# Adding the V bias by a one-row fp32 matmul in PSUM instead of in the VectorE eviction

## The reference, cut to what matters

```python
q = jnp.einsum('bse,hed->bhsd', x, Wq) + bq[None, :, None, :]
kg = jnp.einsum('bse,ged->bgsd', x, Wk) + bk[None, :, None, :]
vg = jnp.einsum('bse,ged->bgsd', x, Wv) + bv[None, :, None, :]
k = jnp.repeat(kg, per, axis=1)
v = jnp.repeat(vg, per, axis=1)
scores = jnp.einsum('bhqd,bhkd->bhqk', q, k) * (1.0 / np.sqrt(d))
# causal mask, softmax -> attn
out = jnp.einsum('bhqk,bhkd->bhqd', attn, v)
```

## Time and profile before

| | us |
|---|---|
| median of 2 runs | 2894.66 (2894.64 to 2894.69) |
| the profiled execution | 2895.81 |
| its span on the slowest core, core 0 | 2894.3 |
| spans of the eight cores | 2878.8 to 2894.3 |
| TensorE busy in the span (matmuls) | 1705.7 |
| ScalarE busy | 1090.4 |
| VectorE busy | 805.1 |

### The profile page before, as it was taken

One profiled execution on the slowest core, in us unless ns is written; L12 is line 12 of the kernel. 1 busy time (PEld: TensorE's weight loads), 2 busy tenths in 40 slices (PEclk: granted clock), 3 DMA queues, 4 the chain that ended last, 5 costly groups with the idle time before them and its releaser, 6 DMA issues.

```text
span 2894.3 us, 19813 instructions; the slowest of 8 cores (2878.8 to 2894.3 us)
## 1 busy us (share of the span) xinstructions
PE 1705.7 (59%) x6824; PEld 722.2 (25%) x6824; DVE 805.1 (28%) x1243; ACT 1090.4 (38%) x1040; POOL 62.2 (2%) x120
## 2 busy tenths in 40 slices
PE   0186565544434434444415888887888848788780
PEld 0033122211112112111103333333333323333330
DVE  0011000123222223223455444444444420000014
ACT  2241000599999999999451000000000000110116
POOL 0000000000000000000000000000000000000000
PEclk9998777756556556556557999999999978898895
DMA  9995322354554555555423333333333341111102
GB/s 225 264 286 132 53 36 37 102 198 169 184 190 170 188 195 174 176 189 170 150 88 117 116 117 116 117 116 117 116 111 120 117 157 39 59 57 41 59 20 116
DMA packets 50741, 376.58 MB, mean 130 GB/s; under 512 B 5588, under 2 KB 5844, under 8 KB 16724
## 3 DMA queue, kind: packets, MB, share of 16 engines
q1 hardware_dynamic: 23188, 192.32, 18.8%
q0 software_dynamic: 17088, 115.35, 14.3%
q10 hardware_dynamic: 10368, 67.64, 7.4%
HBM read 361.13 MB, written 39.32 MB: 138 GB/s over the span
## 4 chain that ended last, share of the span: by engine, by line
PE 28%; DMA 23%; ACT 19%; DVE 13%; issue 11%; another core or an unknown queue 5%; ACTq 1%; SPq 0%; DVEq 0%; POOL 0%; POOLq 0%
DMA af<-w_sb 15%; PE pH L978 12%; ACT L520 8%; DVE ab L827 7%; ACT ab L520 4%; DMA ab<-wq_sb 4%; DVE ab L824 4%; DMA ab<-w2qs 3%; ACT L399 3%; PE psB L330 1%; PE psO L330 1%; PE pH L864 1%; PE psA L330 1%; PE psR L330 1%
## 5 line engine op out<-in xcount | busy, mean ns | idle before, releaser
L864 PE MATMUL pH<-ab 128*128 128x512 bf16 x2752 | 647.7, 398 | 144.1 <-DVE ab L836 108.9
L520 ACT ACT_TABLE_LOAD x256 | 328.4, 1283 | 350.1 <-PE psA L466 309.4
L864 PEld LDWEIGHTS pH<-ab 128*128 128x128 bf16 x2752 | 275.7, 102 | 515.8 <-issue 230.9
L978 PE MATMUL pH<-ab 128*128 128x512 bf16 x1376 | 334.4, 409 | 100.2 <-DMA ab<-w2qs 100.2
L878 ACT ACTIVATE af<-pH,af 128x1024 f32<-128x1024 f32 x43 | 47.9, 1115 | 709.6 <-DVE ab L836 702.1
L824 DVE TENSOR_SCALAR ab<-af 128x2048 bf16<-128x2048 f32 x86 | 110.6, 1286 | 404.6 <-DMA af<-w_sb 404.6
L555 DVE TENSOR_TENSOR ab<-ab 128x128 bf16<-128x128 bf16 x256 | 57.5, 225 | 581.4 <-ACT ab L520 581.4
L978 PEld LDWEIGHTS pH<-ab 128*128 128x128 bf16 x1376 | 141.9, 104 | 289.0 <-issue 150.6
L827 DVE SCALAR_TENSOR_TENSOR ab<-af,ab 128x2048 bf16<-128x2048 f32 x86 | 202.3, 2352 | 9.0
L466 PE MATMUL psA<-ab 128*128 128x512 bf16 x192 | 75.8, 458 | 199.0 <-ACT ab L520 195.9
L466 PE MATMUL psB<-ab 128*128 128x512 bf16 x192 | 75.2, 455 | 167.1 <-ACT ab L520 167.0
(11 more groups left out here) (102 smaller groups left out, 1276.4 us busy)
## 6 DMA issues: line engine op xcount, KB each, us to landing
af<-w_sb POOLq DMA_DIRECT2D x86, 1024.0 KB, 5.3
af<-w_sb SPq DMA_DIRECT2D x86, 1024.0 KB, 5.0
af<-w_sb ACTq DMA_DIRECT2D x64, 688.0 KB, 5.2
af<-w_sb ACTq DMA_DIRECT2D x8, 2752.0 KB, 20.8
af<-w_sb SPq DMA_DIRECT2D x8, 2752.0 KB, 20.9
w2qs<-ab SPq DMA_DIRECT2D x16, 1376.0 KB, 8.5
ab<-w2qs SPq DMA_DIRECT2D x16, 1376.0 KB, 5.9
ab<-xkvT POOLq DMA_DIRECT2D x8, 1024.0 KB, 108.3
```

Of the source, the lines that this page charges most:

```text
L520: INC(scalar.activation(abf(A_PT + OFF[kc], N), ps[:, 0:N], AF.Exp, bias=m16col), "ex", 1)
L864: last = tensor.matmul(ps[:, b2 * 512:(b2 + 1) * 512], lhs, abf(A_XKV + ec * 1024 + b2 * 512, 512), start=(ec == 0), stop=(ec == NEC - 1))
L978: last = tensor.matmul(ps[:, b2 * 512:(b2 + 1) * 512], lhs, abf(A_G + hc * 1024 + b2 * 512, 512), start=(hc == 0), stop=(hc == NHC - 1))
```

## The change

The bias is no longer added in the eviction. A new DRAM input `bvf` (1x512 fp32) is loaded by SP, as a fourth constant counted on `ld`, into one partition of `af` at column offset `F_FSC`. Nothing else uses these columns until FFN part B. Each V unit begins with a matmul of a single contraction row: `onesrow` (1x128 fp32, all ones) is stationary and `bvf` (1x512 fp32) moves. It writes the bias to all 128 partitions of the unit's PSUM bank, with `start=True`. The 16 bf16 matmuls then accumulate on it (`start=False` throughout). The first V unit also waits for `ld`. The eviction becomes a VectorE `tensor_copy`. The bf16 replica of the bias leaves `constb`, whose size stays at 768 columns. The bias is now added in fp32 rather than rounded to bf16 first.

```diff
+    d_bv = nc.dram_tensor("bvf", [1, 512], F32, kind="ExternalInput").ap()
...
-        bvrep = abf(A_CBF + 256, 512)
...
             INC(sync.dma_start(out=abf(A_MSK, 2048), in_=d_msk), "ld", 16)
+            INC(sync.dma_start(out=af[0:1, F_FSC:F_FSC + 512], in_=d_bv), "ld", 16)
         on("sync", p0_sync)
...
-            def mk_mm(tt=tt, ps=ps):
+            def mk_mm(tt=tt, ps=ps, first=(tt == 0)):
                 def mm(tensor):
+                    if first:
+                        W(tensor, "ld", LD_CONSTS)
+                    tensor.matmul(ps[:, 0:512], onesrow,
+                                  af[0:1, F_FSC:F_FSC + 512],
+                                  start=True, stop=False)
                     last = None
                     for ec in range(NEC):
                         lhs = abf(A_XKV + ec * 2048 + tt * 128, 128)
                         last = tensor.matmul(ps[:, 0:512], lhs,
                                              abf(A_WV + ec * 512, 512),
-                                             start=(ec == 0), stop=(ec == NEC - 1))
+                                             start=False, stop=(ec == NEC - 1))
...
             def mk_ev(tt=tt, ps=ps):
                 def ev(vector):
-                    return vector.tensor_tensor(
-                        abf(A_VTM + tt * 512, 512), ps[:, 0:512],
-                        bvrep, ALU.add)
+                    return vector.tensor_copy(abf(A_VTM + tt * 512, 512),
+                                              ps[:, 0:512])
```

More of the change, by code:

```diff
@@ L1058, in _host_shared @@
     constf[:, F_EPS] = 1e-5
-    bv_cat = np.concatenate([bv[g] for g in range(GG)])
+    bv_cat = np.ascontiguousarray(
+        np.concatenate([bv[g] for g in range(GG)]).reshape(1, 512), dtype=f32)
     constb = np.zeros((128, 768), dtype=ml_dtypes.bfloat16)
@@ L1063, in _host_shared @@
     constb[:, 128:256] = np.float32(1.0)
-    constb[:, 256:768] = np.broadcast_to(bv_cat[None, :], (128, 512)).astype(
-        ml_dtypes.bfloat16)
     masks = []
@@ L1084, in _host_shared @@
     return dict(wq_sb=wq_sb, wk_sb=wk_sb, wv_sb=wv_sb, w1_sb=w1_sb, w3_sb=w3_sb,
-                w2_sb=w2_sb, constf=constf, constb=constb), masks
+                w2_sb=w2_sb, constf=constf, constb=constb, bvf=bv_cat), masks
 def kernel(L0_attn_x, L0_attn_Wq, L0_attn_bq, L0_attn_Wk, L0_attn_bk,
```

## The result

The changed kernel takes 0.78% longer: the ratio to the kernel before is 1.0078, with a 95% interval of 1.0066 to 1.0089. On 2894.28 us, the median of the kernel before in that comparison, that is 22.6 us more (19.1 to 25.8). The forecast was 13.8 us more, with the time between 2901 and 2914 us. So the direction and the small size were right, while the price was under two thirds of the measured one, and the time lies above the range. The nine executions behind the ratio go from 2913.3 to 2928.0 us; their median, 2914.5, is 20.3 us more and half a microsecond above the range. By the 2% bound the change is "same".

The account below looks back on a forecast made before the run. TensorE's unbroken V units, which gate the loads for Q, were taken as the bound. TensorE +13.8, eviction 0 and constants 0 us on the 2894.66 us median gave 2908.5 us, range 2901 to 2914 us.

Parts of the forecast that it names:

- What bounds the stage: In the V units TensorE works without idle time; a microsecond added to one moves the loads for Q and the rest.
- The eviction and the added load: VectorE's V eviction without its addition, and SP's extra 2 KB constant load: each forecast at 0 us on the path.
- Two instructions for each call, twice the bf16 time for each: Each new fp32 matmul heading a V unit: two instructions of 2 x 0.216 us, 0.86 us, 13.8 us for 16.
- The dear reading: Skill's transpose sentence read as four times the fp32 transposes' price per column, in one instruction: 28 us for 16 matmuls.
- The joins: Where bf16 matmuls and the new fp32 one meet in a V unit: no exposed weight load counted in the sum.
- the fourth of "What is added to TensorE": Bounds on the 16 new matmuls' price in the V units: 6.9 us lowest, 17.3 with exposed loads, 27.6 us upper.
- the bound for exposed loads: Both fp32 weight loads of 0.11 us exposed in each V unit: 3.5 us on top of 13.8, 17.3 us.
- Nothing given back or added later: After the V units, the loads for Q keep their 36.6 us and later stages only move, their lengths unchanged.
- exposed loads or dear columns: Rival, chance 0.17: the new matmuls in the V units cost between +17.3 and +27.6 us, total 2912 to 2922 us.
- The clock rival: Rival, chance 0.03: TensorE's clock falls to 1.2 GHz for the V units, +83 us, 2977.6 us.
- the input arrives sooner: Rival, chance 0.02: a later `w2` stream speeds the input, so time doesn't grow; it would need 13.8 us.
- the sign of 1 us around 160 us: Forecast counts as wrong if the input's last piece comes more than 1 us away from 160 us.

## Why the prediction was right or wrong, point by point

- **What bounds the stage**: right. TensorE's own time sets the end of the V units, and each microsecond there moves the loads for Q and what follows: 18.5 us more in the V units, 18.5 and 18.7 us more up to the first Q matmul. (The 33.31 us of the earlier trace rows are the last piece of that wait; from the end of the V units to the first Q matmul it is 36.6, which the sum uses.)
- **The eviction and the added load**: right, at nothing, shown by the run without the matmul. The copy costs what the addition did, 692 ns, the bound of the two at which nothing is saved.
- **Two instructions for each call, twice the bf16 time for each**: right. The full-height fp32 matmul costs 0.858 us against the forecast 0.86. The Trainium skill ("FP8 and Floating Point Precision", TensorE Precision Notes) states that true fp32 makes four passes; the 3.97 bf16 times in the table above agree with it. The dear reading, 28 us, didn't come.
- **The joins**: this step failed, the fourth of "What is added to TensorE". The sum took them at nothing, because a full-height fp32 load starts under the bf16 matmul ahead of it. The rows were right and the inference wrong: they show another type at the same height, and the new matmul differs in height as well. At full height the forecast came true to 0.1 us (13.73 against 13.8). At one row 0.30 us were added to each, 4.8 us in all, and a V unit lasted 4.61 us, over the 4.5 named as a sign of being wrong. Even the bound for exposed loads, 17.3 us, was short of 18.5: it counted the two fp32 loads at 0.11 us each, whereas one load and two waits of some 0.09 us around the change of height were lost.
- **Nothing given back or added later**: right for the loads for Q, and not quite for the rest. FFN part A was 4.2 us longer on either chip, which the sum had at nothing and the prediction named as a sign of being wrong. Its cause is open, and it isn't tied to the number of new matmuls.
- **The rivals**: "exposed loads or dear columns" came, with a chance of 0.17, at 18.5 us of its 17.3 to 27.6. Its mechanism was the right one, loads that stand exposed for another height; the prediction had itself noted that no row shows a one-row load ahead of a 128-row matmul in a dense stream. The clock rival didn't come: 1.00 through the V units. Whether the input arrives sooner can't be told to the microsecond: the V units start at 211.2 and 208.1 us in two profiles of the kernel before, and at 207.6 and 207.2 in two of the changed one. So the sign of 1 us around 160 us, named in the prediction, tells nothing.
- **The range** ended at 2914 us, inside the exposed case. The joins alone give 2894.7 + 18.5 = 2913.2 us, which is inside it. The measured 2917 us lies 3.7 us above that, and FFN part A is the only later stage that was longer on both chips. The spread of later stages between programs should have widened it by some us.

## What to carry to other kernels

Price a small matmul put into a dense stream by its streaming, plus a join where the operands' height changes and changes back (0.21 us in bf16 and 0.30 us in fp32 here); look for a row with the same height and type as the neighbours before taking a weight load as hidden. If a bias must go through PSUM, a full-height bf16 matmul costs a fifth of the one-row fp32 one (0.216 against 1.156 us, with the bias rounded to bf16), and an addition in an eviction that already waits for TensorE costs nothing (VectorE waited 2.8 us before each one here). And read the gap behind the stage that is being edited: here the waits between the Q units, with the clock that they cost, were worth 113 us, against 18.5 us for the row.

## What the runs showed of the hardware

- A one-row weight load among full-height ones isn't pulled ahead of the matmul before it, and neither is the full-height load that follows: 0.21 us for each pair of changes in bf16 and 0.30 us in fp32, at a granted clock of 1.00. Between two one-row fp32 matmuls nothing is lost (the second costs 0.859 us).
- An fp32 matmul of 512 columns streams in 0.858 us at full height, 3.97 times the 0.216 us of bf16, in two recorded instructions. A change of type alone loses nothing: at full height fp32 adds 13.73 us in 16 units, 0.858 for each.
- A VectorE copy from PSUM of 128x512, fp32 to bf16, takes 692 ns, as the addition of a bf16 tile does.
- The same stage, unedited, differs between programs by up to 8 us of 810 (805.1 to 813.4), and repeats within 1.1 and 2.8 us for the same program.
- 32 matmuls of 128x512 in bf16 take 8.5 to 10.0 us where a gap of 5.7 to 6.7 us comes before them (granted clock 0.78 over that stretch) and 6.91 us where none does.
